# Cross attention that divides its output for two units at once, norms a group two slots later and drains the last outputs ahead of the class ranks

## The reference

```
x = layernorm(x + self_attention(x))        # 8 heads of 16, blocks of 64 tokens, biases
x = layernorm(x + cross_attention(x, ctx))  # 16 heads of 8, mask, no biases
x = layernorm(x + experts(x))
# experts: logits = x @ Wr.T (8 experts); top 2 of softmax, weights renormalized;
# each expert is W2 @ silu(W1 @ x), hidden width 512
```

## Time and profile before

| what | us |
|---|---|
| median of 3 runs (range) | 1175.23 (1173.22 to 1178.68) |
| the profiled execution's own time | 1175.13 |
| its span | 1173.3 |
| PE, DVE, ACT, POOL busy | 940.2, 854.6, 712.7, 432.5 |
| mean granted TensorE clock | 0.896 of full speed |

### The profile page before, as it was taken

How to read it: one execution, slowest core, us unless ns; L and a number is a source line. 1 busy time by engine, 2 the same in 40 slices (tenths; PEclk the granted TensorE clock), 3 DMA queues, 4 the chain that set the end, 5 groups by cost and what they waited for, 6 DMA issues and landing times. The chain is left out here.

```text
span 1173.3 us, 31174 instructions
## 1 busy us (share of the span) xinstructions
PE 940.2 (80%) x11091; PEld 835.9 (71%) x11092; DVE 854.6 (73%) x2668; ACT 712.7 (61%) x1193; POOL 432.5 (37%) x527
## 2 busy tenths in 40 slices
PE   3888888888789989898989897685009999999991
PEld 2677776777678778787878686574009999999991
DVE  3687878788878888888888886666605767776772
ACT  3666667576477766666766556342007777877781
POOL 3142423324410111111111123543262777777674
PEclk9898889898899998999999979796559999999996
DMA  5940000000001000000000000000012322332220
GB/s 162 210 69 19 18 9 18 9 18 18 13 13 24 13 13 13 13 11 11 11 11 11 12 5 22 31 22 17 10 55 62 69 67 67 70 70 61 51 44 0
DMA packets 103727, 42.26 MB, mean 36 GB/s; under 512 B 58291, under 2 KB 99517, under 8 KB 103669
## 3 DMA queue, kind: packets, MB, share of 16 engines
q1 hardware_dynamic: 98676, 32.94, 13.8%
q0 software_dynamic: 4992, 8.54, 2.3%
HBM read 20.68 MB, written 16.57 MB: 32 GB/s over the span
## 5 line engine op out<-in xcount | busy, mean ns | idle before, releaser
L897 ACT ACTIVATE pr<-psum 128x512 f32<-128x512 f32 x192 | 114.1, 594 | 107.7 <-PE psum L604 102.7
L1107 DVE TENSOR_TENSOR at<-psum,rc 64x32 f32<-64x32 f32 (+1 forms) x768 | 153.5, 200 | 14.4
L1091 DVE TENSOR_REDUCE mx<-psum 128x8 bf16<-128x512 f32 x192 | 132.9, 692 | 36.3 <-PE psum L525 23.7
L901 ACT ACTIVATE pt<-psum 128x512 f32<-128x512 f32 x192 | 113.2, 589 | 66.9 <-PE psum L613 62.9
L501 POOL DMA_INDIRECT out_dram<-X,dest x92 | 122.8, 1335 | 65.1 <-ACT X L999 47.0
L613 PE MATMUL psum<-ident,pr 128*128 128x128 f32 x768 | 127.1, 291 | 14.8 <-ACT pr L897 11.5
L629 PE MATMUL psum<-vz_cross,pt 128*128 128x36 f32 x1024 | 133.2, 278 | 0.0
L629 PEld LDWEIGHTS psum<-vz_cross,pt 128*128 128x128 f32 x1024 | 131.3, 201 | 0.2
L604 PE MATMUL psum<-mx,negI 128*128 128x512 bf16 x192 | 77.4, 403 | 50.8 <-DVE mx L1091 46.8
L613 PEld LDWEIGHTS psum<-ident,pr 128*128 128x128 f32 x768 | 93.5, 151 | 29.5 <-ACT pr L897 20.7
L378 POOL TENSOR_SCALAR ve<-mv 128x4 f32<-128x4 f32 x55 | 19.5, 355 | 241.3 <-DVE mv L1241 224.6
(11 more groups left out here) (220 smaller groups left out, 3137.9 us busy)
## 6 DMA issues: line engine op xcount, KB each, us to landing
xd<-blank SPq DMA_DIRECT2D x1, 6072.0 KB, 37.5
X<-xd SPq DMA_DIRECT2D x23, 264.0 KB
X<-x_dram SPq DMA_DIRECT2D x16, 256.0 KB, 2.9
wst<-w_dram SPq DMA_DIRECT2D x16, 256.0 KB, 2.7
cin<-ctx_in_dram SPq DMA_DIRECT2D x16, 256.0 KB, 2.8
out_dram<-X,dest POOLq DMA_INDIRECT x92, 2.3
mraw<-mask_dram SPq DMA_DIRECT2D x32, 32.0 KB, 2.7
xd<-XTa,pos POOLq DMA_INDIRECT x64, 2.3
```

The lines of the kernel that those rows point to most:

```text
L897: nc.scalar.activation(pr[u % 2][:], SC[u % 2][:], ACT.Exp).then_inc(s["ex"], 1)
L901: nc.scalar.activation(pt[u % 2][:], TB[u % 2][:], ACT.Copy).then_inc(s["ph"], 1)
L1091: nc.vector.tensor_reduce(mx[u % 2][:], SC[u % 2][:].rearrange("p (r k) -> p r k", k=S), AX.X, ALU.max).then_inc(s["mx"], 1)
L1107: m = nc.vector.tensor_tensor(dst, src, r, ALU.mult)
```

## The change

In cross attention only:

- **Pair norm.** Two units share a bank: values(u) writes to columns 0 to 143 or 144 to 287 of PVB[u // 2 % 2]. norm runs in even slots alone, for two units: one reciprocal 128x32, four multiplies 64x64. values of an even unit waits for the pair norm two before it, odd ones for none; the semaphore nm counts pairs.
- **Finish** moves from the end of slot 5 to the end of slot 7 (FIN), there ahead of select. Stats stay in slot 5.
- **POOL.** convert moves from ahead of the scatters to behind inv_std. Of the scatters of groups 13, 14 and 15, 6, 7 and 7 (8, 9 and 9 before) stand ahead of inv_std. low_rows(14) goes ahead of the last inv_std.
- **Slots.** RT 4 to 3; rank 2 to 3, its reader of_class and own_rank in slot 4; logits 6 to 5, keep still in 6. `lead` is now columns 288 on of both banks. The tables of group 12 move: whole, capacity and the first placement to slot 6, the second to slot 7. The matmul of the totals becomes count, with a semaphore of its own.
- **Close.** values, RT(14), AT(15), rank(6), logits(14), O(15), ...; VectorE norm first, class ranks ahead of stats.

```diff
-        lead = PVB[1][:, 144:]
+        lead = [PVB[1][:, 288:], PVB[0][:, 288:]]
...
                     stage(g, i, s["xs"], s["xt"])
-                    if la.cross:
-                        convert(g, i)
...
                         inv_std(g - 1, s["mv"], before, s["rs"])
+                    if la.cross and follow >= 2:
+                        convert(g + 2, i)
...
                 def groups():
                     over_groups(la, pool, body)
+                    if la.cross:
+                        low_rows(G - 2)
                     inv_std(G - 1, s["mv"], before, s["rs"])
...
-                    wait(pe, s["nm"], n - 1)
+                    if not la.cross:
+                        wait(pe, s["nm"], n - 1)
+                        dst = PVB[u % 2]
+                    else:
+                        if u % 2 == 0:
+                            wait(pe, s["nm"], g * (la.nh // 2) + u // 2 - 1)
+                        dst = PVB[u // 2 % 2][:, u % 2 * HB * W:]
...
                 def AT(g, i):
-                    pe.wait_ge(s["nm"], (g + 1) * la.nh)
+                    pe.wait_ge(s["nm"], (g + 1) * (la.nh // 2 if la.cross else la.nh))
...
                 def closing():
+                    last_values()
                     RT(G - 2, G)
-                    last_values()
+                    AT(G - 1, 1)
                     rank(NPAIR - 2, last_rk[0])
                     logits(G - 2, last_lg[0])
-                    last_out()
+                    O(G - 1, 1)
                     RT(G - 1, G)
                     logits(G - 1, last_lg[1])
-                    rank(NPAIR - 1, last_rk[1], True)
+                    pe.wait_ge(r_s, PT * NPAIR)
+                    count(last_rk[1][:, PT * NP:])
+                    rank(NPAIR - 1, last_rk[1])
...
                 def norm(g, u, i):
-                    n = g * la.nh + u
+
                     quad, half = us[u]
-                    dve.wait_ge(s["pv"], n + 1)
-                    pv = PVB[u % 2][:, 0:HB * W].rearrange("p (b jc e) -> p b jc e", b=HB, jc=4)
-                    nc.vector.reciprocal(rc[u % 2][:], pv[:, :, :, la.dk]).then_inc(s["rc"], 1)
+                    many = 2 * HB if la.cross else HB
+                    dve.wait_ge(s["pv"], g * la.nh + u + 1)
+                    n = g * (la.nh // 2) + u // 2 if la.cross else g * la.nh + u
+                    k = (u // 2 if la.cross else u) % 2
+                    raw = PVB[k][:, 0:many * W]
+                    recip = rc[k][:, 0:many]
...
-                        if u > 0:
-                            norm(g, u - 1, i)
-                        elif not first:
-                            norm(g - 1, la.nh - 1, 1 - i)
+                        if not la.cross or u % 2 == 0:
+                            if u > 0:
+                                norm(g, u - 1, i)
+                            elif not first:
+                                norm(g - 1, la.nh - 1, 1 - i)
...
-                        if u == slot(la, "O") + 1 and not first:
+                        if u == slot(la, "FIN") and not first:
                             finish(g - 1)
                     if route and i == 1:
                         select(p - 1)
...
                 def closing():
+                    last["norm"]()
                     rl(G - 2)
-                    last["norm"]()
                     last["al"]()
-                    last["stats"]()
                     of_class(NPAIR - 2, last_rk[0])
                     own_rank(NPAIR - 2)
+                    last["stats"]()
...
-SENT_BEFORE = {12: range(0), 13: range(4, 12), 14: range(15, 24), 15: range(28, 37)}
-SENT_AFTER = {12: range(0, 4), 13: range(12, 15), 14: range(24, 28), 15: range(37, 40)}
-SLOTS = {"self": {"QK": 0, "V": 1, "AT": 1, "O": 2, "XT": 3},
-         "cross": {"QK": 0, "V": 2, "AT": 3, "O": 4, "XT": 5, "CT": 6, "HIGH": 1, "RANK": 2, "OWN": 3, "RT": 4, "LG": 6}}
+SENT_BEFORE = {12: range(0), 13: range(4, 10), 14: range(15, 22), 15: range(28, 35)}
+SENT_AFTER = {12: range(0, 4), 13: range(10, 15), 14: range(22, 28), 15: range(35, 40)}
+SLOTS = {"self": {"QK": 0, "V": 1, "AT": 1, "O": 2, "XT": 3, "FIN": 3},
+         "cross": {"QK": 0, "V": 2, "AT": 3, "O": 4, "XT": 5, "CT": 6, "FIN": 7, "HIGH": 1, "RT": 3, "RANK": 3, "LG": 5}}
```

More of the change, by code:

```diff
@@ L138, in program @@
         mx = [sb(f"mx{i}", [P, 8], BF16) for i in range(2)]
-        rc = [sb(f"rc{i}", [P, HB, 4], F32) for i in range(2)]
+        rc = [sb(f"rc{i}", [P, GB, 4], F32) for i in range(2)]
         at = [sb(f"at{i}", [P, GT, D], F32) for i in range(2)]
@@ L438, in opening @@
                         pool.wait_ge(sems["self"]["fin"], 2)
-                    ahead(0, 0)
-                    ahead(1, 1)
+                    for g in range(2):
+                        ahead(g, g)
+                        if la.cross:
+                            convert(g, g)
                 def body(g, i, follow, p):
                     route = la.cross and not (isinstance(g, int) and g < 2)
-                    late = la.cross and isinstance(g, int) and g >= GA + 2
+                    late = la.cross and isinstance(g, int) and g >= first_tables
                     if route:
@@ L479, in _ @@
             next_groups()
-            for h in range(G - 2, G):
-                low_rows(h)
+            low_rows(G - 1)
             pool.wait_ge(r_lr, G)
             pool.wait_ge(r_pos, 4)
-            send(range(GA * GT, NT))
+            send(range(chunk(1).start, chunk(1).stop))
             def take(j, i):
@@ L669, in logits, with count, rank @@
                     m.then_inc(r_lg, 1)
-                def rank(p, dst, total=False):
+                def count(dst):
+                    nc.tensor.matmul(totals(dst), ones2[:, 0:P], S16[:, PT - 1, :], start=True, stop=True, skip_group_check=True).then_inc(r_count, 1)
+                def rank(p, dst):
                     pe.wait_ge(r_s, PT * (p + 1))
@@ L675, in rank @@
                     m = nc.tensor.matmul(flat, ones2[:, 0:P], S16.rearrange("p t c -> p (t c)"), start=False, stop=True, skip_group_check=True)
-                    if total:
-                        m = nc.tensor.matmul(totals(dst), ones2[:, 0:P], S16[:, PT - 1, :], start=True, stop=True, skip_group_check=True)
                     m.then_inc(r_rank, 1)
@@ L1134, in body @@
                     ranked = la.cross and i == 0 and not (isinstance(g, int) and g < 4)
-                    tables = la.cross and isinstance(g, int) and g == GA + 2
+                    tables = la.cross and isinstance(g, int) and g == first_tables
                     for u in range(la.nh):
@@ L1253, in _ @@
             lane_rows = cst[:, o + 3 * NP:o + 3 * NP + 1]
-            room, start, ends, more, shifted, ones_c, past, past_b = (tab[:, n] for n in (0, 1, 2, 4, 5, 6, 7, 8))
-            ends_both = tab[:, 2:4].rearrange("p n c -> p (n c)")
-            past_both = tab[:, 7:9].rearrange("p n c -> p (n c)")
+            room, start, more, shifted, ones_c = (tab[:, n] for n in (0, 1, 5, 6, 7))
+            ends = [tab[:, 2 + c] for c in range(2)]
+            past = tab[:, 8]
+            ends_all, past_all = (tab[:, n:n + 2].rearrange("p n c -> p (n c)") for n in (2, 8))
             def each(v):
@@ L1490 @@
     const[:, o:o + NP] = rows - 9 * E
-    const[:, o + NP:o + 2 * NP] = np.append(np.diff(rows), rows[0] - rows[-1])
-    const[:, o + 2 * NP:o + 3 * NP] = np.append(np.diff(rows), 0)
+    steps = [np.append(np.diff(rows), last) for last in [rows[0] - rows[-1]] * 1 + [0]]
+    const[:, o + NP:o + 3 * NP] = np.concatenate(steps)
     const[:, o + 3 * NP] = np.arange(P) * P
```

87 lines of the change are left out of this document (47 added, 40 removed).

## The result

The changed kernel took **1144.66 us** (median of 4 runs, 1141.35 to 1145.64) beside 1176.95 of the kernel before in the same series: a ratio of 0.9719 with an interval of 0.9675 to 0.9762. The forecast was 1151.8, from 1140 to 1168. Direction and range held; the gain was larger, 31.1 us between the two spans (1173.3 and 1142.2) in place of 23.3. How much of that agreement is the mechanism and how much is luck is taken up behind the experiments.

A forecast was written before the change was run, and what follows sets the result against it. TensorE (308 of 339 us busy) and VectorE (292) lie close together mid cross attention, so the order of work decides. Terms summed to -23.3 from 1175.1, giving 1151.8 us, range 1140 to 1168.

The forecast's parts named there:

- Slots 6 and 7: Groups 1 to 11 of cross attention: all 21 TensorE waits for VectorE's maximum in these slots go, -14.9 us.
- Ahead of the maximum after a selection: Four TensorE pauses after selections each grow by 1.17 us, +4.7; group 12's wait for the gates' exponential grows, +1.0.
- pauses of 3.3 to 3.6: Sign that the forecast is right: TensorE's pauses after selections last 3.3 to 3.6 us.
- Group 12: VectorE leads because of the tables; relief between 0 and 3.8 us, not all arriving because of the placements: -2.5 us.
- Group 13: Fewer scatters ahead of inv_std end the 9.08 us wait; -9.1 and -0.9, pause after selection +2.2: net -7.8 us.
- Group 14: Loses its waits of 0.88 and 0.48 us for a maximum: -1.4 us.
- Closing: Last group's end: norm first, AT without waiting for rank, O starts earlier: -2.4 us, bounds -1 and -3.
- A: Rival: waits of slots 6 and 7 stay because maxima there wait for scores; 1170.6 us, chance 0.09.
- D: Rival: in group 13 inv_std stays late behind the later scatters; 1159.6 us, chance 0.06.
- C: Rival: the pair's multiply costs per short run, so norm saves nothing; slower, 1184 us, chance 0.05.
- B: Rival: longer pauses hold TensorE's clock down, six pauses costing 15 us more; 1167 us, chance 0.10.
- The rule on the shared port: VectorE's finish would wait for GpSimd scatters in groups 12 to 15; not counted, 3.7 us as bound, giving 1155.5.

The follow-up runs named there:

- division alone: Changed kernel with routing slots, finish (slot 5), GpSimd's order and closing all as before, so only the pair division is new: 1135.58 us, ratio 0.9900 to the kernel before.
- first pair: Changed kernel and kernel before in the first series, no further edit: 1144.66 us beside 1176.95, ratio 0.9719.
- closing back: Changed kernel with the old closing order on TensorE and VectorE, and GpSimd's low rows of group 14 behind inv_std: 1115.38 us, ratio 0.9760 to the kernel before.
- second pair: Kernel before and changed kernel each run once more, no edit: 1170.41 us and 1141.45 us, ratio 0.9723.
- GpSimd's order back: Changed kernel with the mask converted behind the staging copy and 8, 9, 9 scatters ahead of inv_std again: 1114.95 us, ratio 0.9743 to the kernel before.
- split in three: Changed kernel with a selection's 16 steps cut: 4 behind slot 6, 5 behind slot 7, 7 behind the next group's first maximum: 1124.66 us, ratio 0.9604.
- division undone: Changed kernel with cross attention again dividing one unit at a time, the moved finish and new orders kept: 1125.04 us, ratio 0.9837 to the kernel before.
- routing slots back: Changed kernel with RT, RANK and LG back in slots 4, 2 and 6: 1102.10 us, ratio 0.9624 to the kernel before.

## Why the prediction was right, and where the sum was off

- **Slots 6 and 7 (-14.9): mechanism right, size and share off.** All 21 waits went. Worth more, because each costs its idle time and 0.17 us: 21 of them 3.6 us more. The moved routing slots gave 0.18 a group, 2.0 us, where nothing was counted. And the forecast let the narrower division carry the first of each pair of maxima and charged the finish only for the pauses. The experiments show the finish's move as the larger part, 1.1 to 1.3 us a group against 0.6 to 0.8. It pays for the 1.03 even in groups with a selection, where both together give 1.8.
- **Ahead of the maximum after a selection (+4.7, and +1.0 in group 12): too large.** The pauses went from 1.89, 2.46, 2.44 and 2.08 to 2.64, 3.21, 3.20 and 3.21, 3.4 in all, and group 12's by 0.58. The sign that was set for it, pauses of 3.3 to 3.6, was not met. The 1.03 of the finish is exact where nothing else changes. With the division alone the first three of the old pauses fall by 0.26 to 0.29, although its norm is wider; that they had held some lateness from slot 7 is argued from these sizes, not shown.
- **Sum of groups 1 to 11.** Forecast -9.2. With the sizes above -14.9, -3.6, -2.0, +3.4 and +0.6 make -16.5. Measured where the clock is alike: the six groups at full clock in all traces give -10.5, group 9 by the same sizes -1.8, and groups 4, 6, 8 and 10 about -1.1 to -1.3 each (as group 6 did at 0.93 in both kernels), some -17 in all, an estimate. The clock then added 4 to 5 us of gain in the first pair (-21.6) and took about 1 in the second (-16.1).
- **Group 12 (-2.5): too small, and not separated.** Measured -5.3 and -4.8. The forecast bounded it by the 3.8 us of the division; the finish out of slot 5 is missing from that bound. But the clock moved too, from 0.76 to 0.94. The division alone took 32.50 us there at 0.95, against 35.3 before, and the kernel with the closing back 29.89 at 0.94. So some 2.6 at nearly the same clock belong to the rest of the change, and how the other 2.8 share out between division and clock is open.
- **Group 13 (-7.8): mechanism right, the size partly luck.** Finish no longer waits for rstd. The second pair gives -7.9, the kernel with GpSimd's order back 6.1 of it. But in the second pair stalls stand in the group, which takes 31.0 us there and 28.3 without them (closing back); and the pause after its selection came to 2.6 and 2.7 us, where 3.4 was put into the sum. In the first pair only 3.2 arrived, since stalls of all engines fell into this group of the changed kernel and its clock was 0.82, against 0.94 in the second.
- **Group 14 (-1.4): not met.** Both pairs give -0.5. In both traces of the changed kernel TensorE still waits 1.5 us for a maximum late in the group; in two kernels of the calls without stalls such a wait is 0.7.
- **Closing (-2.4): right.** 2.9 alone. The whole traces show 5.0 and 5.2; that the rest came with stalls in group 15 is argued, from 98 and 93 us for this stretch in the traces with stalls against 88.9 and 86.0 without.
- **The whole.** The 1144.7 us lie nearer to the forecast than its terms do: groups 1 to 11 gave twice their forecast, and a start 4.1 us later and the stalls in group 13 took some of it back. That part of the agreement is luck.
- **Rivals.** A (waits stay), D (deviation late) and C (multiply per short run) are refuted by the rows above; for C, 222 ns. B (longer pauses hold the clock down) is not borne out in size: some 1 us in the second pair, and in the first the low level was rarer than before, with the same pauses. What the forecast charged for the low level, half of its time, is too much for a short stretch of it: 24.5, 25.2, 26.8 and 28.1 us for an even group at 1.00, 0.93, 0.87 and 0.82 are 0.7, 2.3 and 3.6 us lost, where half the time would be 1.8, 3.5 and 5.1. (The 24.5 is group 4, which is 0.2 shorter than group 6 at full clock in the split in three.)
- **The rule on the shared port** would have made finish slower beside the scatters, and the forecast put nothing for it. For the changed kernel that held: in both of its traces the finish of groups 12 to 15 took 1.11 or 1.12 us for its four instructions, as in the earlier trace rows. But the collision is there in other kernels. Beside the cast of the mask the finish takes 1.39 us, as shown above. Beside a scatter it takes 1.34 in the last groups of three kernels, and that scatter 1.16 in place of 0.96:

```profile
759.94 1.34 DVE L1268 TENSOR_SCALAR X<-z,mv,rstd 128x128 f32<-128x128 f32 x4
760.10 1.16 POOL L424 DMA_INDIRECT xd<-XTa,pos  x1 [0.20 <-issue]
```

The largest is the finish of the last group wherever the closing is the old one, the kernel before included:

```profile
765.90 1.14 POOL L404 TENSOR_TENSOR XTa<-X,XTa 128x512 f16<-128x512 f32 x1
765.95 1.95 DVE L1270 TENSOR_SCALAR X<-z,mv,rstd 128x128 f32<-128x128 f32 x4 [0.76 <-POOL rstd L382]
```

Four instructions take 1.95 us there and 1.11 in the kernels where the low rows come earlier. The Trainium skill (SBUF — State Buffer, Who interferes with whom) says that the later of two such instructions waits for the whole of the first; the 0.84 us more agree in direction, and are less than the 1.14 of the first. The new order of the closing avoids it.

## What to carry to other kernels

When two engines are close together, list what stands on the late engine ahead of each maximum that the other waits for, and price each piece by the wait that it lengthens in *its* slot. Here a piece of 1.1 us that was only moved, to where its engine had idle time, was worth more in the middle groups than the 3.4 us of work that was taken away; and one slot too little between a producer and its reader cost everything. Look also at what a moved piece now meets on another engine: the finish and GpSimd's cast, side by side, cost 0.28 us a group. Long strings of small steps are best cut and laid into idle slots, but then look who reads their result: the queue behind it, GpSimd's here, moves with it.

## What the runs showed of the hardware

**Stalls in some calls and not in others.** In groups 12 to 15, which are written out and not looped, TensorE, VectorE and ScalarE stop together with the releasers "issue" or "remote". Between 640 and 790 us the traces of the two slower calls and of the first pair show 8 to 17 such idle times of 0.8 us or more (23.0 to 43.8 us, the three engines added); the seven traces of the two faster calls show none, whatever the kernel. The two slower calls were on one chip, the faster ones on two others, so chip and call are not told apart further. Between 325 and 640 us no trace has one.

This one

```profile
731.77 0.69 DVE L1110 TENSOR_REDUCE mx<-psum 128x8 bf16<-128x512 f32 x1 [6.70 <-remote]
```

is from the changed kernel's second trace. Groups 13 and 14 take 28.3 and 26.4 us where there are none (closing back), 31.0 and 34.7 in that trace. Groups 0 to 3 are written out too and show none, so that alone is not the cause. Where these stalls come from was not tried.

**The clock after a pause is no function of its length.** After two pauses of 3.21 us in the changed kernel's second trace the lower level held for 7 us and for over 9, with TensorE busy throughout:

```profile
544.00:551.00 7.00, 7.00 (x50) 6.21 (x49) 5.83 (x13) 4.64 (x8) 2.64 (x6) 0.53 0.00 0
600.00:609.00 9.00, 9.00 (x58) 7.80 (x58) 5.38 (x13) 5.55 (x11) 2.64 (x6) 0.50 0.00 0
```

With the division alone the three pauses of 2.17 to 2.18 us are followed twice by full clock (groups 6 and 8, 25.2 us) and once by the lower level (group 10, 27.6 us at 0.88). With the division undone, pauses of 3.11 give the lower level in groups 6 and 8 and full clock in group 10. The two traces of the changed kernel differ by 5.5 us over eleven groups, all of it in groups with a different clock.

**The reciprocal** took 249 ns for 16 and 352 for 32 columns from PSUM, 6.4 ns for each column more, where the multiply that goes from 32 to 64 columns costs 33 ns more.

**Open.** The routing slots back have a lower ratio (0.9624) than the changed kernel (0.9723), though their groups are 0.2 us longer. The two ran on different chips. The trace of the first also reached the stage earliest of all (group 1 at 349.2 us) and has the highest mean clock, 0.926; the two were not set side by side, so whether the moved routing slots help the whole kernel is open.
